# A mixture-of-experts FFN on one core: the hardware loops over experts and over weight tiles are written out

## The chip, the core and the metric

The kernel runs on one core of one Trainium2 chip. The metric is device time in microseconds of one execution; lower is better. A core has five engines that run their own instruction streams side by side and meet at semaphores: TensorE (PE, matrix multiplies), VectorE (DVE), ScalarE (ACT), GpSimd (POOL) and SyncE (SP, which here only issues transfers).

## What is computed

Each of 4096 tokens (512 wide) is rotated by a 4x4 quaternion product. A gate picks the best 2 of 8 experts, each expert takes at most 1024 tokens in order of arrival, and an expert is a two-layer FFN (512 to 2048 with relu, 2048 to 512). The weighted results are added to the input.

```python
xr = hamilton(q_left_n, hamilton(x_filtered, q_right_conj))      # spectral gate is a factor
scores = softmax(xr @ gate_w.T); topv, topi = top_k(scores, 2)
gates = topv / sum(topv)
loc = place of the token in its expert; valid = loc < cap         # cap = 1024
disp[topi * cap + loc] += xr * valid
h  = relu(einsum('ecd,ehd->ech', disp, fc1_w) + fc1_b)
eo = einsum('ech,ehd->ecd', h, fc2_w) + fc2_b
out = x + sum(eo[flat_idx] * gates * valid)
```

## The kernel before

**Two parts.** A straight part of about 105 us loads x, computes the gate, sorts tokens into the 8 x 1024 slots and prepares the first slab. Then comes the main part: 8 experts, in each 2 slabs of 512 slots (`half`), in each 16 steps (`hh`, one 128-row tile of the hidden layer). That is 256 steps in all, 32 to an expert.

**One step on PE.** Every product is done in three fp32r pieces (hi x hi, hi x lo, lo x hi). A step of PE is `fc1` for the step after it (12 matmuls into `hp`, lines 830 to 832) and then `fc2` for the step itself (12 matmuls into the accumulators `eo`, lines 842, 843 and 847). The very last step has only `fc2`. A matmul here is a weight load (PEld in the profile) and a multiply.

**The others in a step.** ACT turns `hp` into `h_hi` (line 448) and `h_full` (line 451), DVE makes `h_lo` of them (line 669). In 16 of the 32 steps of an expert ACT and DVE also prepare a weight tile two steps ahead: DVE turns it (`turn_tile`, line 656), ACT rounds it to `w1T_hi` and `w2_hi` (lines 438, 440), and DVE makes the remainders `w1T_lo` and `w2_lo` (lines 661, 664). After the last step of a slab DVE adds the four blocks of `eo` to `rows` (line 765), and POOL scatters them to `out` (line 385). POOL gathers the next slab's rows, ACT issues transfers that bring them through DRAM, and DVE rotates them.

**The loops.** PE, DVE, ACT and POOL each run the function `expert(e, last)` through the helper `experts` of lines 237 to 241: experts 0 to 6 in a hardware loop (`Fori`, a register counts `e`), and then expert 7 as straight code. So each of these four engines has six jumps back from the end of an expert to the start of the body, and one place, between experts 6 and 7, where it runs on into straight code. SP has a hardware loop of its own (line 278): the loads of weight tiles 2 to 127, two tiles to an iteration, each load waiting until its buffer is free (`w1_T`, `w2_ready`). Where a wait or an address depends on `e` or `m`, it is a register that an instruction (REGISTER_ALU) has computed; in straight code it is a constant.

**Order.** All orders are written out by hand and enforced by semaphores. Nothing in the kernel uses a scheduler.

Of the kernel before, what the change touches and what calls it, by code (L numbers as in the profile page):

```python
# [34 lines left out]
def program(nc, x, cond, q_right, spectral, gate_w, fc1_w, fc1_b, fc2_w, fc2_b, out):  # L35
    B, S, D = x.shape
    E, H, _ = fc1_w.shape
# [5 lines left out]
    HT = H // P  # L43
# [7 lines left out]
    RAW = 2  # L51
# [30 lines left out]
    with ctx:  # L82
# [153 lines left out]

        def experts(eng, body):

            with eng.Fori(0, E - 1) as e:
                body(e, False)  # L240
            body(E - 1, True)

        def load_cut(eng, to, rows_128, arrived, parts=range(P // BLK)):

            cut = rows_128.rearrange("(hq r) (k dq c) -> dq r k hq c", r=BLK, k=Q, c=BLK)
            for dq in parts:
                part = to[dq * BLK:(dq + 1) * BLK, :].rearrange("r (k hq c) -> r k hq c", k=Q, c=BLK)
                eng.dma_start(part, cut[dq]).then_inc(arrived, 16)  # L250
# [3 lines left out]
        @block.sync  # L254
        def _(sp):
            sp.dma_start(small[0:Q, :], cond).then_inc(small_in, 16)
            sp.dma_start(small[Q:2 * Q, :], q_right).then_inc(small_in, 16)
            sp.dma_start(small[2 * Q:2 * Q + 1, :], spectral.rearrange("a b c d -> (a b c) d")).then_inc(small_in, 16)
            sp.dma_start(gw_nat[:, :], gate_w).then_inc(gw_in, 16)
            for q in range(Q):  # L260
                sp.dma_start(x_all[:, 0:XC, q * P:(q + 1) * P], x_tiles[:, 0:XC, q * P:(q + 1) * P]).then_inc(x_in0[q], 16)
            sp.dma_start(b1_nat[:, :], fc1_b.rearrange("e a (t p) -> (e a t) p", p=P)).then_inc(b1_in, 16)
            for c in range(1, CHUNKS):
                tiles = slice(XC * c, XC * (c + 1))
                sp.dma_start(x_all[:, tiles, :], x_tiles[:, tiles, :]).then_inc(x_in[c][0], 16)
            def load_w1(row, c):

                load_cut(sp, w1_raw[:, c, :], w1_rows[ds(row, P), :], w1_in[c])

            for n in range(RAW):  # L270
                load_w1(n * P, n)
                sp.dma_start(w2_raw[:, n, :], w2_rows[n * P:(n + 1) * P, :]).then_inc(w2_in[n], 16)
            for c in range(CHUNKS):
                tiles = slice(XC * c, XC * (c + 1))
                for arrived in x_in[c]:
                    sp.wait_ge(arrived, 16)
                sp.dma_start(out_tiles[:, tiles, :], x_all[:, tiles, :]).then_inc(out_init, 16)
            with sp.Fori(1, E * HT // RAW) as m:
                for c in range(RAW):
                    sp.wait_ge(w1_T, RAW * m + (c - RAW + 1))  # L280
                    load_w1(m * (RAW * P) + c * P, c)
                    sp.wait_ge(w2_ready, RAW * m + (c - RAW + 1))
                    sp.dma_start(w2_raw[:, c, :], w2_rows[ds(m * (RAW * P) + c * P, P), :]).then_inc(w2_in[c], 16)

        @block.gpsimd
        def _(pool):
# [86 lines left out]
            def expert(e, last):  # L373
                for half in range(SLABS):
# [22 lines left out]
                    if not (last and half >= SLABS - 2):  # L397
                        gather_x(s + 2, half, 1)

            experts(pool, expert)  # L400

        @block.scalar
        def _(act):
# [68 lines left out]
            def expert(e, last):  # L472
                for half in range(SLABS):
                    for hh in range(HT):
# [15 lines left out]
                        if not end:  # L490
# [13 lines left out]
                            if hh in HI_AT:  # L504
                                split_y(s1, (half + 1) % 2, HI_AT.index(hh))

            experts(act, expert)

        @block.vector
        def _(dve):  # L510
# [218 lines left out]
            def expert(e, last):  # L729
                for half in range(SLABS):  # L730
                    s = e * SLABS + half
                    end = last and half == SLABS - 1
                    for hh in range(HT):
# [27 lines left out]
                        if hh == HT - 1:  # L761
                            for b in range(SB):
# [3 lines left out]
                                                         rows[:, b, :], ALU.mult, ALU.add).then_inc(sums_ready, 1)  # L766

            experts(dve, expert)

        @block.tensor  # L770
# [139 lines left out]
```

## Time and profile before

| | before |
|---|---|
| time, median of 3 runs | 1538.37 us (1534.41 to 1542.68) |
| span of the profiled execution | 1528.3 us |
| what lies around the span, median minus span | 10.1 us |
| PE busy | 1458.1 us, 95% of the span |
| DVE, ACT, POOL busy | 820.2, 537.3, 285.5 us (54%, 35%, 19%) |
| mean granted TensorE clock | 0.977 of full speed |
| instruction transfers | 69 packets on q8, 41 on q14 |

The profiled execution's own total time is not among the three; its span is from the first to the last instruction, and the median lies 10.1 us over it. The profile divides time by engine and by source line, and for each instruction it says how long its engine had sat idle before it and what ended that. "issue" there is time in which the engine waited for nothing that the profile shows. PE's records overlap, since matmuls are pipelined: one is 390 ns long, but one starts every 227 ns.

### The profile page before, as it was taken

What the parts mean: (1) busy time and instruction counts of PE and PEld (TensorE: products, weight loads), DVE (VectorE), ACT (ScalarE), POOL (GpSimd) and SP (SyncE); (2) the same over time, 40 slices, a digit from 0 to 9 for tenths busy, and PEclk for the clock granted to TensorE, in tenths of its full rate; (3) what the DMA queues carried; (4) which work ended last, traced back from release to release, by engine and by line L of the source; (5) the groups of instructions that cost most, each with busy time, mean ns of one, the idle gap of its engine ahead of it and who ended that gap; (6) DMA issues with size and microseconds to landing.
All of it is one profiled execution on the core that took longest, in us unless ns stands there. A gap on an engine that the chain in (4) does not pass through costs nothing.

```text
span 1528.3 us, 21024 instructions
## 1 busy us (share of the span) xinstructions
PE 1458.1 (95%) x6470; PEld 1196.0 (78%) x6470; DVE 820.2 (54%) x1484; ACT 537.3 (35%) x871; POOL 285.5 (19%) x342
## 2 busy tenths in 40 slices
PE   7569999999999999999999999999999999999996
PEld 5348888788887888788887888788887888888885
DVE  6756634575355824566345753568245662558311
ACT  4234422343233422344233432344223432344221
POOL 1040030301204031120303121130312103030301
PEclk9669999999999999999999999999999999999998
DMA  8456431774319732394318742296324943196100
GB/s 291 179 138 146 100 102 36 160 146 106 75 41 180 151 97 55 96 175 98 110 28 160 159 103 65 53 190 134 91 55 107 174 90 103 34 181 137 56 0 27
DMA packets 446304, 169.30 MB, mean 111 GB/s; under 512 B 405248, under 2 KB 407433, under 8 KB 444274
## 3 DMA queue, kind: packets, MB, share of 16 engines
q1 hardware_dynamic: 293218, 84.01, 25.7%
q0 software_dynamic: 18096, 52.35, 12.1%
q10 hardware_dynamic: 134880, 31.47, 10.1%
q8 instruction: 69, 1.13, 0.3%
q14 instruction: 41, 0.34, 0.1%
HBM read 127.00 MB, written 41.03 MB: 110 GB/s over the span
## 4 chain that ended last, share of the span: by engine, by line
PE 95%; DVE 2%; issue 1%; DMA 0%; POOL 0%; ACT 0%; SPq 0%; DVEq 0%; POOLq 0%
PE hp L831 15%; PE hp L830 15%; PE eo L843 15%; PE eo L842 15%; PE eo L847 15%; PE hp L832 15%; PE hp L855 1%; PE eo L805 1%; PE hp L787 1%; PE hp L788 1%; DVE y_half L713 0%; DVE x_turned L713 0%; DMA rows<-in_x,gather_row 0%; PE xp L794 0%; DVE yT_lo L698 0%
## 5 line engine op out<-in xcount | busy, mean ns | idle before, releaser
L669 DVE TENSOR_TENSOR h_lo<-h_full,h_hi 128x512 fp32r<-128x512 f32 x256 | 176.6, 690 | 537.7 <-ACT h_full L451 537.6
L831 PE MATMUL hp<-yT_lo,w1T_hi 128*128 128x512 f32 x1020 | 397.7, 390 | 16.3 <-issue 16.3
L830 PE MATMUL hp<-yT_hi,w1T_hi 128*128 128x512 f32 x1020 | 398.1, 390 | 0.4 <-issue 0.2
L842 PE MATMUL eo<-w_hi,h_hi 128*128 128x512 f32 x1024 | 398.3, 389 | 0.0
L843 PE MATMUL eo<-w_lo,h_hi 128*128 128x512 f32 x1024 | 398.3, 389 | 0.0
L832 PE MATMUL hp<-yT_hi,w1T_lo 128*128 128x512 f32 x1020 | 397.5, 390 | 0.0
L448 ACT ACTIVATE h_hi<-hp,b_now 128x512 fp32r<-128x512 f32 x256 | 176.1, 688 | 617.7 <-PE hp L832 613.0
L847 PE MATMUL eo<-w_hi,h_lo 128*128 128x512 f32 x1024 | 273.7, 389 | 0.0
L832 PEld LDWEIGHTS hp<-yT_hi,w1T_lo 128*128 128x128 f32 x1020 | 192.0, 188 | 57.3 <-issue 17.6
L830 PEld LDWEIGHTS hp<-yT_hi,w1T_hi 128*128 128x128 f32 x1020 | 191.8, 188 | 42.1 <-issue 2.4
L842 PEld LDWEIGHTS eo<-w_hi,h_hi 128*128 128x128 f32 x1024 | 192.3, 188 | 40.0
L847 PEld LDWEIGHTS eo<-w_hi,h_lo 128*128 128x128 f32 x1024 | 192.2, 188 | 39.9
L843 PEld LDWEIGHTS eo<-w_lo,h_hi 128*128 128x128 f32 x1024 | 192.2, 188 | 39.9
L831 PEld LDWEIGHTS hp<-yT_lo,w1T_hi 128*128 128x128 f32 x1020 | 191.9, 188 | 39.6
L438 ACT ACTIVATE w1T_hi<-w_turned 128x512 fp32r<-128x512 f32 x128 | 80.8, 631 | 273.3 <-DVE w_turned L656 258.3
L451 ACT ACTIVATE h_full<-hp,b_now 128x512 f32<-128x512 f32 x256 | 174.5, 682 | 0.0
L348 POOL DMA_INDIRECT x_blk<-in_x,gather_now x60 | 61.3, 1022 | 553.8 <-DVE x_turned L677 542.4
L385 POOL DMA_INDIRECT out<-rows,scatter_now x64 | 65.2, 1018 | 515.9 <-DVE rows L765 504.0
L692 DVE SCALAR_TENSOR_TENSOR y_half<-x_turned,rot,y_half 128x256 f32<-128x256 f32 x360 | 150.0, 478 | 0.0
L661 DVE TENSOR_TENSOR w1T_lo<-w_turned,w1T_hi 128x512 fp32r<-128x512 f32 x128 | 88.6, 693 | 92.4 <-ACT w1T_hi L438 92.4
L656 DVE STREAM_TRANSPOSE w_turned<-w_raw 128x512 f32<-128x512 f32 x126 | 88.7, 704 | 16.2 <-issue 9.5
L664 DVE TENSOR_TENSOR w_lo<-w_raw,w_hi 128x512 fp32r<-128x512 f32 x128 | 87.6, 684 | 10.2 <-ACT w_hi L440 10.1
(146 smaller groups left out, 717.0 us busy)
## 6 DMA issues: line engine op xcount, KB each, us to landing
w_raw<-in_L_ffn_fc_w SPq DMA_DIRECT2D x512, 64.0 KB
w_raw<-in_L_ffn_fc_w SPq DMA_DIRECT2D x128, 256.0 KB, 3.1
slots_dram<-x_blk ACTq DMA_DIRECT2D x30, 512.0 KB, 3.6
x_blk<-slots_dram ACTq DMA_DIRECT2D x240, 64.0 KB
out<-x_all SPq DMA_DIRECT2D x8, 1024.0 KB, 12.3
x_all<-in_x SPq DMA_DIRECT2D x7, 1024.0 KB, 13.9
b_bc<-in_L_ffn_fc_b POOLq DMA_DIRECT2D x8, 256.0 KB
x_all<-in_x SPq DMA_DIRECT2D x4, 256.0 KB, 4.1
```

Of the source, the lines that this page charges most:

```text
L448: act.activation(h_hi[:, c, :], hp[:, c, :], ACT.Relu, bias=b1_now[:, hh:hh + 1]).then_inc(h_hi_ready, 1)
L451: act.activation(h_full[:, :], hp[:, c, :], ACT.Relu, bias=b1_now[:, hh:hh + 1]).then_inc(h_full_ready, 1)
L656: dve.transpose(w1_turned[:, c, :, :].rearrange("p q n -> p (q n)"), w1_raw[:, c, :]).then_inc(w1_T, 1)
L661: dve.tensor_tensor(w1T_lo[:, hh, :, :], w1_turned[:, c, :, :], w1T_hi[:, hh, :, :].bitcast(F32), ALU.subtract).then_inc(w1_ready, 1)
L669: dve.tensor_tensor(h_lo[:, c, :], h_full[:, :], h_hi[:, c, :].bitcast(F32), ALU.subtract).then_inc(h_ready, 1)
L692: ins = dve.scalar_tensor_tensor(y, x_turned[:, :, j, :], rot[:, i, j:j + 1], y, ALU.mult, ALU.add)
L830: pe.matmul(bank, w1T_hi[:, hh, q, :], yT_hi[:, par, q, :], start=(q == 0), stop=False)
L831: pe.matmul(bank, w1T_hi[:, hh, q, :], yT_lo[:, par, q, :], start=False, stop=False)
L832: ins = pe.matmul(bank, w1T_lo[:, hh, q, :], yT_hi[:, par, q, :], start=False, stop=(q == Q - 1))
L842: pe.matmul(eo[:, b, :], h_hi[:, c, blk], w2_hi[:, hh, :], start=(hh == 0), stop=False)
L843: pe.matmul(eo[:, b, :], h_hi[:, c, blk], w2_lo[:, hh, :], start=False, stop=False)
L847: pe.matmul(eo[:, b, :], h_lo[:, c, blk], w2_hi[:, hh, :], start=False, stop=(hh == HT - 1)).then_inc(fc2_done, 1)
```

## The change

The two `Fori` loops become Python loops, so that the program holds the body of every expert on every one of the four engines, and the 63 iterations of SP's loads. Order, buffers and waits are the same; wait values and addresses that were registers are constants. Straight code has no branch in the main part.

```diff
         def experts(eng, body):
 
-            with eng.Fori(0, E - 1) as e:
+            for e in range(E - 1):
                 body(e, False)
             body(E - 1, True)
...
-            with sp.Fori(1, E * HT // RAW) as m:
+            for m in range(1, E * HT // RAW):
                 for c in range(RAW):
                     sp.wait_ge(w1_T, RAW * m + (c - RAW + 1))
                     load_w1(m * (RAW * P) + c * P, c)
```

On PE, where an expert's body ends and the next begins, before (the two L239 rows are the loop counter and the jump; the rows behind them are the straight code of expert 7, and the jump's target starts with the same matmuls):

```order
L844 REGISTER_ALU
L847 MATMUL eo<-w2_hi,h_lo 128x512 x4
L239 REGISTER_ALU
L239 COMPARE_AND_BRANCH
L830 MATMUL hp<-yT_hi,w1T_hi 128x512
L831 MATMUL hp<-yT_lo,w1T_hi 128x512
```

and the same place now, as it stands at every expert:

```order
L842 MATMUL eo<-w2_hi,h_hi 128x512
L843 MATMUL eo<-w2_lo,h_hi 128x512
L847 MATMUL eo<-w2_hi,h_lo 128x512 x4
L830 MATMUL hp<-yT_hi,w1T_hi 128x512
L831 MATMUL hp<-yT_lo,w1T_hi 128x512
```

No matmul moved; the jump and the register instructions are gone. On DVE, at the same place of the program, before:

```order
L763 REGISTER_ALU
L764 REGISTER_ALU
L765 SCALAR_TENSOR_TENSOR rows<-eo,gate_now,rows 128x512
L239 REGISTER_ALU
L239 COMPARE_AND_BRANCH
L656 STREAM_TRANSPOSE w1_turned<-w1_raw 128x512
L661 TENSOR_TENSOR w1T_lo<-w1_turned,w1T_hi 128x512
```

and now:

```order
L669 TENSOR_TENSOR h_lo<-h_full,h_hi 128x512
L765 SCALAR_TENSOR_TENSOR rows<-eo,gate_now,rows 128x512 x4
L656 STREAM_TRANSPOSE w1_turned<-w1_raw 128x512
L661 TENSOR_TENSOR w1T_lo<-w1_turned,w1T_hi 128x512
```

The four sums of a slab and the turn of the next expert's third weight tile now follow each other without a jump. The program's PE code grows from 1,860 to 6,468 matmuls, DVE's, ACT's and POOL's code by a factor of about 2.5, and SP's from 44 to 664 transfers.

## Rows read from the trace of the kernel before

**Rows 1.** The page, part 1: busy time, share and instructions of each engine

```profile
PE 1458.1 (95%) x6470; PEld 1196.0 (78%) x6470; DVE 820.2 (54%) x1484; ACT 537.3 (35%) x871; POOL 285.5 (19%) x342
```

**Rows 2.** The page, part 4: the chain that ended last, by engine

```profile
PE 95%; DVE 2%; issue 1%; DMA 0%; POOL 0%; ACT 0%; SPq 0%; DVEq 0%; POOLq 0%
```

**Rows 3.** Waits: engine and line, releaser, us in total, times, longest

```profile
ACT h_hi L448 <- PE hp L832: 613.0, 224, 4.2
...
PE hp L831 <- issue: 16.3, 6, 2.9
...
DVE w_turned L656 <- issue: 9.5, 6, 1.8
...
DVE w_turned L656 <- DMA w_raw<-in_L_ffn_fc_w: 6.7, 6, 2.2
```

**Rows 4.** Timeline of PE, first jump back (start, us, what, idle before)

```profile
278.07 1.07 PE L847 MATMUL eo<-w_hi,h_lo 128*128 128x512 f32 x4
...
280.02 0.40 PE L830 MATMUL hp<-yT_hi,w1T_hi 128*128 128x512 f32 x1
282.82 0.59 PE L831 MATMUL hp<-yT_lo,w1T_hi 128*128 128x512 f32 x1 [2.40 <-issue]
283.20 0.63 PE L832 MATMUL hp<-yT_hi,w1T_lo 128*128 128x512 f32 x1
...
288.01 1.07 PE L847 MATMUL eo<-w_hi,h_lo 128*128 128x512 f32 x4
```

**Rows 5.** Timeline of PE, second jump back

```profile
456.65 1.07 PE L847 MATMUL eo<-w_hi,h_lo 128*128 128x512 f32 x4
457.87 0.49 PE L830 MATMUL hp<-yT_hi,w1T_hi 128*128 128x512 f32 x1
...
461.95 0.39 PE L831 MATMUL hp<-yT_lo,w1T_hi 128*128 128x512 f32 x1 [2.89 <-issue]
...
465.59 0.62 PE L847 MATMUL eo<-w_hi,h_lo 128*128 128x512 f32 x2
```

**Rows 6.** Timeline of PE: step 0, and experts 6 to 7, run on without a jump

```profile
109.43 1.07 PE L847 MATMUL eo<-w_hi,h_lo 128*128 128x512 f32 x4
...
1343.10 1.07 PE L847 MATMUL eo<-w_hi,h_lo 128*128 128x512 f32 x4
1344.01 0.39 PE L830 MATMUL hp<-yT_hi,w1T_hi 128*128 128x512 f32 x1
...
1349.44 0.39 PE L830 MATMUL hp<-yT_hi,w1T_hi 128*128 128x512 f32 x1
...
1514.46 1.07 PE L847 MATMUL eo<-w_hi,h_lo 128*128 128x512 f32 x4
```

**Rows 7.** Stretches: us, busy of PE, PEld, DVE, ACT, POOL, granted clock, DMA share, GB/s

```profile
278.00:292.00 14.00, 11.51 (x44) 8.87 (x43) 7.89 (x12) 3.65 (x7) 6.13 (x8) 0.88 0.70 195
292.00:1515.00 1223.00, 1208.71 (x5327) 999.00 (x5326) 645.75 (x1149) 432.03 (x698) 230.65 (x255) 1.00 0.48 104
```

**Rows 8.** DMA queues, stretch 459.3 to 461 us: packets, MB, share of 16 engines

```profile
q8 instruction: 1, 0.02, 4.3%
```

**Rows 9.** DMA queues, stretch 1343 to 1515 us, expert 7

```profile
q8 instruction: 6, 0.10, 0.2%
q14 instruction: 3, 0.02, 0.1%
```

**Rows 10.** Timeline of DVE, second jump back

```profile
457.18 2.73 DVE L765 SCALAR_TENSOR_TENSOR rows<-eo,gate_now,rows 128x512 f32<-128x512 f32 x4
461.51 0.71 DVE L656 STREAM_TRANSPOSE w_turned<-w_raw 128x512 f32<-128x512 f32 x1 [1.61 <-issue]
```

**Rows 11.** Timeline of DVE, experts 6 to 7, run on without a jump

```profile
1343.62 2.73 DVE L765 SCALAR_TENSOR_TENSOR rows<-eo,gate_now,rows 128x512 f32<-128x512 f32 x4
1346.27 0.70 DVE L656 STREAM_TRANSPOSE w_turned<-w_raw 128x512 f32<-128x512 f32 x1
1347.67 0.69 DVE L661 TENSOR_TENSOR w1T_lo<-w_turned,w1T_hi 128x512 fp32r<-128x512 f32 x1 [0.70 <-ACT w1T_hi L438]
```

**Rows 12.** Timeline of SP's queue and of DVE, one load and what frees its buffer

```profile
446.15 0.70 DVE L656 STREAM_TRANSPOSE w_turned<-w_raw 128x512 f32<-128x512 f32 x1
...
447.04 2.89 SPq L250 DMA_DIRECT2D w_raw<-in_L_ffn_fc_w  x4
```

## The prediction

> **What bounds the kernel now.** I read the busy times first, then the chain that ended last, then PE's waits, and then PE's timeline around the places where the loop jumps back. PE is busy 1458.1 us of a span of 1528.3 [rows 1], and the chain is PE for 95% [rows 2]. So the only time to be had without removing matmuls is time in which PE stands. In the main part PE has exactly one kind of wait: before line 831, "issue", 6 times, 16.3 us together, 2.9 at the longest [rows 3]. Six is the number of jumps back. All six stand at the same place: four matmuls into the first step of the next expert, and not at a semaphore, since line 831 is the second piece of an `fc1` that is already under way. ACT, by contrast, waits for PE's `hp` in 224 of 256 steps, 613.0 us together [rows 3]: it has spare time nearly everywhere, and so has DVE.
>
> **What the jumps cost, from PE's step.** "Idle" understates it, so I count by the period of a step. The L847 groups of step 0 and step 31 start at 109.43 and 278.07 [rows 4, 6]: 168.64 us for 31 steps, 5.440 us each. Expert 7, which is straight code already, shows the same: from the L847 of step 223 (1343.10) to that of step 255 (1514.46) there are 171.36 us [rows 6], which is 32 x 5.440 less the 2.72 of the `fc1` that the last step lacks, to the hundredth. In between, from step 31 (278.07) to step 223 (1343.10), there are 192 steps: 192 x 5.440 = 1044.5, but they take 1065.0. The surplus is **20.5 us**, over the six jumps, 3.4 each. It has three parts.
> - The idle time itself, 16.3.
> - At the first jump the granted clock is 0.88 on average over 14 us [rows 7], and the matmuls right after the pause are 0.63 us long instead of 0.39 [rows 4]. This step pair takes 288.01 - 278.07 = 9.94, that is 4.50 over 5.44, of which 2.40 is idle. Most of the other 2.1 is the slow clock. In the 1223 us after that, with five more jumps, the clock is 1.00 [rows 7].
> - At the other jumps a few tenths around the pause: the second takes 465.59 - 456.65 = 8.94, that is 3.50 over a step, of which 2.89 is idle; the first matmul behind the jump starts 1.22 after the L847 group instead of 0.91 [rows 5, 6]. I take 2.1 for all five, what is left of the 20.5.
>
> **What the pause is.** In the stretch of 1.7 us that lies within the second pause one packet of 16 KB (0.02 MB) moves on an instruction queue, q8 [rows 8]. I read this as PE's next piece of code: the jump goes to code that is no longer, or only in part, on hand; the first eight instructions (four loads and four multiplies) are there, the next piece is asked for only when it is needed, and PE stands meanwhile. In expert 7 the same queue brings 6 packets in 172 us, one each 28.7, and PE does not pause once [rows 6, 9]. Straight code is evidently fetched ahead.
>
> [...]
>
> **The change, part by part.**
> - *PE's jumps go.* Gain 20.5 us, all of it on the path, if each expert's start now looks like that of expert 7: L847 at 1343.10, `fc1` at 1344.01, 0.91 later, as in any step [rows 6].
> - *PE's register instructions go.* They lie under matmuls; steps are 5.440 us long in the loop and in straight code alike. Gain 0.
> - *PE's code gets longer.* Six more copies of the body, each 32 x 5.440 = 174 us long, are 1044 us of it; at a packet each 172 / 6 = 28.7 us that is some 36 packets. The loop already took such packets while it ran (q8 is used in all experts), and PE's only pauses were the six at the jumps. Cost 0 as in expert 7; the bound above is that of rival D.
> - *DVE's, ACT's and POOL's jumps go.* DVE stands 6 times for 9.5 us together at its jump [rows 3], for instance 1.61 at 461.51 [rows 10]. These lie beside PE's pause and bring nothing by themselves. They matter for what follows: once PE no longer pauses, what these engines do at an expert's start must be in time by itself.
> - *What is late next.* The tightest place is the third weight tile of an expert. DVE may turn it only behind the four sums of the slab. Between experts 6 and 7, where nobody jumps, the sums run from 1343.62 to 1346.35, the turn starts at 1346.27, and `w1T_lo` is done at 1347.67 + 0.69 = 1348.36 [rows 11]. The `fc1` that reads it starts at 1349.44 [rows 6]. The margin is 1.08 us, and PE did not wait. The six other boundaries get this same margin. I cost this at 0; the cover is those 1.08 us, and if it is gone (a weight load that comes late: DVE waited for one 6 times, 2.2 us at most [rows 3]) it costs the excess, up to 1.1 us a time. Expert 7 has less to do than others, but the boundary's own work (sums, tile, `h_hi`, stores) is the same.
> - *SP's loop goes.* The first load of an iteration is issued at 447.04, when DVE's turn that frees its buffer ended at 446.85 [rows 12]; the jump of SP lies within waiting time. Gain 0. No load starts earlier in the step than now, since each still waits for DVE's turn, so no new collisions of transfers.
> - *Head and tail.* The straight part of 105 us and the last 14 us after PE's last step have no loop and stay.
>
> Sum: 0 + 20.5 off the span, 1528.3 - 20.5 = 1507.8. The median stands 10.1 over the span, which nothing here touches: **1517.9 us**, 1.3% faster. The pauses differ between jumps (the shortest and longest of the rows shown are 2.40 and 2.89), and the slow clock behind the first one need not be there in every run: from 16.3 + 2.1 without it to some 24 with a second such case, 1514 to 1520. The three runs spread over 8.3 us, half a per cent, so 1514 to 1522 is the forecast's own range.
>
> **Rivals.**
> - *B, the margin at the boundary does not hold.* For it: 1.08 us is little, and DVE waited up to 2.2 for a weight load. Against it: the one straight boundary showed no wait, and those 6 waits for loads never reached PE. Price up to 2.2 - 1.08 = 1.1 at six boundaries, 6.7 together: 1518 to 1524.6.
> - *C, the pause is not the jump's.* Something at an expert's boundary other than the jump holds PE, or straight code brings its own pause at the same place. Then nothing changes: 1538. Against it: the boundary at 1343.10 has the same work and no pause. [...]
> - *D, slower.* PE's code does not arrive ahead of need once all of it is straight. The place is the end of each piece of 28.7 us; the price at most that of a jump's pause, 2.7 (16.3 / 6), for 36 new pieces: 97 us, and 1615 in the worst case. It outweighs the gain from 20.5 / 36 = 0.57 us a piece. For it: nothing in the rows but that transfers of code share the 16 DMA engines with data, and those are 48% busy in the main part [rows 7]. Against it: six pieces in expert 7 without a pause.
>
> **How the numbers follow.** Forecast (all 20.5, within its spread) 0.78; B 0.12; C 0.05, with the branch-price reading another 0.02; D 0.03. What this kernel's measurement can tell from no change is about 0.5%, 7.7 us: forecast and B lie beyond it (0.90 faster), C within it (0.07), D slower (0.03). The time is the forecast's, 1517.9. The range takes the forecast's spread and B: 1513 to 1525; C and D, 0.10 together, stay out.
>
> **What would show it.** Right: PE's wait "issue" before line 831 gone from the waits; a distance of 1384.5 us between the first and the last L847 group (255 x 5.440 less 2.72; now 1405.0); a span near 1508; a granted clock of 1.00 from 105 us to the end of PE's work; fewer packets on q8 than now, about 1390 / 28.7 = 48 for the main part. B shows as waits of PE for DVE's `w1T_lo` at line 830 at the experts' starts. C shows as the same six pauses; D as short "issue" waits each 28.7 us, or long steps at that distance. The forecast is wrong if PE's step leaves 5.44 us, or if a slower start eats the gain: the first L847 group should still start near 109.4.

## The result and the profile after

| | before | after |
|---|---|---|
| time, median | 1536.39 us (1531.74 to 1542.68, 4 runs) | 1510.70 us (1508.79 to 1511.23, 4 runs) |
| ratio after to before, 95% interval | | 0.9834 [0.9801, 0.9868] |
| span of the profiled execution | 1528.3 us | 1509.3 us |
| mean granted TensorE clock | 0.977 | 0.977 |
| instruction packets on q8, on q14 | 69, 41 | 52, 35 |
| idle time of PE at the starts of experts | 16.3 us, six times | none |

The change makes the kernel 1.7% faster. The sign and the mechanism of the forecast hold. The time does not: 1517.9 was forecast, the range began at 1513, and 1510.7 was measured. The spread is new as well: before ran over some 11 us, after over 2.4.

The page of the kernel after, its part 1 and two lines of its part 3, answering to [rows 1] and [rows 9]:

```profile
PE 1455.4 (96%) x6470; PEld 1196.7 (79%) x6470; DVE 819.8 (54%) x1484; ACT 537.2 (36%) x871; POOL 283.5 (19%) x342
...
q8 instruction: 52, 0.85, 0.2%
q14 instruction: 35, 0.29, 0.1%
```

PE's timeline (start, us, what, idle before): the first and the last L847 group, answering to [rows 6], and the matmuls at the first expert boundary, answering to [rows 4].

```profile
111.00 1.07 PE L847 MATMUL eo<-w_hi,h_lo 128*128 128x512 f32 x4
...
285.08 1.07 PE L847 MATMUL eo<-w_hi,h_lo 128*128 128x512 f32 x4
285.99 0.39 PE L830 MATMUL hp<-yT_hi,w1T_hi 128*128 128x512 f32 x1
...
1495.48 1.07 PE L847 MATMUL eo<-w_hi,h_lo 128*128 128x512 f32 x4
```

From the first group to the last there are 1384.48 us; the prediction had 1384.5 for 255 steps without a pause. No step of the main part is longer than 5.44 us. The stretches (us, busy of PE, PEld, DVE, ACT, POOL, granted clock, DMA share, GB/s) say the same, answering to [rows 7]:

```profile
278.00:292.00 14.00, 14.00 (x63) 11.59 (x63) 9.25 (x14) 6.44 (x11) 5.03 (x6) 1.00 0.77 198
...
105.00:1495.00 1390.00, 1390.00 (x6127) 1151.16 (x6127) 746.44 (x1328) 499.89 (x808) 255.71 (x287) 1.00 0.48 105
```

PE is busy in all 1390 us of the main part. The boundary work on DVE, answering to [rows 11], here for experts 0 to 1:

```profile
280.07 2.73 DVE L765 SCALAR_TENSOR_TENSOR rows<-eo,gate_now,rows 128x512 f32<-128x512 f32 x4
282.71 0.70 DVE L656 STREAM_TRANSPOSE w_turned<-w_raw 128x512 f32<-128x512 f32 x1
284.11 0.69 DVE L661 TENSOR_TENSOR w1T_lo<-w_turned,w1T_hi 128x512 fp32r<-128x512 f32 x1 [0.70 <-ACT w1T_hi L438]
```

`w1T_lo` is done at 284.80 and PE reads it from 285.99 on: a margin of 1.19 us. It is 1.18 or 1.19 at all seven boundaries, so rival B did not happen.

The span fell by 19.0 us, not by the 20.5 that went from the steps, because the main part began 1.57 us later (first group at 111.00 instead of 109.43). The straight part differed: the second half of its first `fc1` began 0.35 us later (102.16 for 101.81), and the clock rose later. Before, a matmul of the first full `fc1` took 0.39 us from 105.33 on (first line); after, matmuls were still 0.63 us long at 107.45 (the others):

```profile
105.33 0.39 PE L832 MATMUL hp<-yT_hi,w1T_lo 128*128 128x512 f32 x1
...
106.17 0.63 PE L830 MATMUL hp<-yT_hi,w1T_hi 128*128 128x512 f32 x1
107.45 0.63 PE L830 MATMUL hp<-yT_hi,w1T_hi 128*128 128x512 f32 x1
108.46 0.40 PE L830 MATMUL hp<-yT_hi,w1T_hi 128*128 128x512 f32 x1
```

This start belongs to the execution, not to the change: in a second profile of the changed kernel (`after_again`) the first L847 group starts at 109.19, and the distance to the last is 1384.47 again.

### The profile page after: what moved, and what is told of

It is laid out like the page before. It is cut to its first block, busy times and chain, and to the rows that moved or that the text cites. A ratio compares the mean times of both kernels' runs of the same rounds, so it can differ in the third digit from the quotient of the medians.

```text
span 1509.3 us, 17949 instructions
## 1 busy us (share of the span) xinstructions
PE 1455.4 (96%) x6470; PEld 1196.7 (79%) x6470; DVE 819.8 (54%) x1484; ACT 537.2 (36%) x871; POOL 283.5 (19%) x342
## 4 chain that ended last, share of the span: by engine, by line
PE 96%; DVE 2%; DMA 1%; POOL 0%; ACT 0%; issue 0%; SPq 0%; DVEq 0%; POOLq 0%
PE eo L842 15%; PE eo L843 15%; PE eo L847 15%; PE hp L830 15%; PE hp L831 15%; PE hp L832 15%; PE hp L855 1%; PE eo L805 1%; PE hp L787 1%; PE hp L788 1%; DMA rows<-in_x,gather_row 0%; DVE x_turned L713 0%; POOL rows L321 0%; POOL out L385 0%; PE xp L794 0%
## 5 line engine op out<-in xcount | busy, mean ns | idle before, releaser
L847 PE MATMUL eo<-w_hi,h_lo 128*128 128x512 f32 x1024 | 273.7, 389 | 0.0
L847 PEld LDWEIGHTS eo<-w_hi,h_lo 128*128 128x128 f32 x1024 | 192.3, 188 | 39.7
L385 POOL DMA_INDIRECT out<-rows,scatter_now x64 | 69.0, 1079 | 517.0 <-DVE rows L765 505.2
## 6 DMA issues: line engine op xcount, KB each, us to landing
out<-x_all SPq DMA_DIRECT2D x8, 1024.0 KB, 11.6
```

The source lines that it names most:

```text
L847: pe.matmul(eo[:, b, :], h_lo[:, c, blk], w2_hi[:, hh, :], start=False, stop=(hh == HT - 1)).then_inc(fc2_done, 1)
```

## Experiments

Theory at the start: the whole gain is PE's six pauses for code and the slow clock behind them. The rival: what was missed lies with the other engines' loops, or outside the span. Three sets of four kernels follow; those of a set ran on one chip beside the kernel of before, whose medians there were 1534.89 (23 runs), 1531.75 (7) and 1532.31 us (7). Every kernel without pauses of 2 us repeats within 5 us, so I compare these by their times. The changed kernel ran beside the first set alone, and the start of the main part moves by up to 2.3 us between executions (first L847 group at 108.74 to 111.00), so a difference of 1 or 2 us between sets means little by itself.

A measure without this is the *surplus*: by how much the distance from the first to the last L847 group, in the profiled execution, is over the 1384.5 us of 255 even steps. It is 20.5 and 22.4 us in the two profiles of before, 21.6 in `others_only`, 9.5 in `head232`, 9.0 in `pair`, 6.3 in `head208`, 4.6 in `pe_only`, 2.7 in `hint`, 2.3 in `head0`, 2.2 in `dve_loop`, and 0.0 in the two profiles of after, in `rest_loop` and in `head0_dve`.

### Before, again: where its spread comes from

The kernel is unchanged.

> The kernel of before, unchanged, for the time and clock of each of its executions. The forecast missed by 5 us on the side of the gain although the span of the profiled execution fell by 19.0, near the 20.5 that was summed. Theory T (clock after a pause): executions of before differ because each of the six pauses may or may not be followed by a few us at the half clock; then span and mean granted clock move together: spans from about 1528 (clock 0.977, one slow stretch behind a pause) up to about 1541 (clock near 0.970, five or six slow stretches of 3.4 us, some 2 us each), and time minus span is the same 1.9 us as in the executions of after. Theory S (outside the span): spans are all near 1528 with clock 0.977, and time minus span varies from 3 to 14 us.

Measured: 1533.93 us (1531.85 to 1542.28, 12 runs), ratio 1.0001 [0.9980, 1.0021]. Theory S is refuted: in all 35 executions of before on that chip, and in every other execution whose span is on record (101 in all), time minus span is 1.6 to 2.1 us. The spans themselves range from 1527.3 to 1540.3. So the profiled execution of the prediction, with a span of 1528.3, took about 1530.2 us, an estimate from its span, since its time isn't on record: it was one of the fastest of this kernel. The "10.1 us around the span" set it against three other executions.

Theory T holds in part. The two executions at clock 0.971 took 1540.6 and 1542.3 us, the three at 0.977 took 1529.2, 1531.6 and 1533.4. In this kernel's profile two of the six pauses are followed by a slow stretch, in the earlier one it was one: a granted clock of 0.50 for 3.4 us, there from 282.8 to 286.1 us, here in 814.2 to 817.5 and 995.1 to 998.4 (windows; columns as above):

```profile
812.00:826.00 14.00, 11.32 (x45) 9.20 (x44) 6.91 (x11) 4.84 (x8) 7.75 (x10) 0.88 0.73 197
990.00:1004.00 14.00, 10.78 (x42) 8.60 (x41) 6.16 (x10) 4.44 (x8) 6.88 (x10) 0.88 0.68 203
```

But executions at clock 0.975 run from 1529.2 to 1540.2, so something besides the clock varies. The same profile shows one such thing, a few steps behind the fifth pause: SP's and ACT's transfers stand for some microseconds, ACT stands 6.4 us before an `h_hi`, and PE, which is hardly ever caught up with, waits for it. One step then takes 5.96 us (1016.06 - 1010.10) instead of 5.44, and the `fc1` behind it waits for its weight tile.

```profile
1010.10 1.07 PE L847 MATMUL eo<-w_hi,h_lo 128*128 128x512 f32 x4
1014.16 0.47 PE L842 MATMUL eo<-w_hi,h_hi 128*128 128x512 f32 x1 [0.27 <-ACT h_hi L448]
...
1016.06 1.07 PE L847 MATMUL eo<-w_hi,h_lo 128*128 128x512 f32 x4
1017.38 0.50 PE L830 MATMUL hp<-yT_hi,w1T_hi 128*128 128x512 f32 x1 [0.26 <-DVE w1T_lo L661]
```

The two steps add 1.1 of the 22.4 us of surplus. How often this happens I can't say from single profiles.

### After, again

The kernel is the changed one.

> The changed kernel once more, beside the others on the same chip. Both theories: median 1508 to 1512 us, ratio to before 0.980 to 0.987. Theory T: no pause, so no slow stretch in the main part, clock 0.977 in every execution and a spread of 3 us at most. Theory S would let it spread as before does, by 8 us or so, since what lies outside the span is the same in both kernels.

Measured: 1510.31 us (1509.41 to 1510.47, 6 runs), ratio 0.9833 [0.9807, 0.9858], clock 0.977 to 0.978. As T expected: without pauses there is neither a slow stretch nor a spread.

### PE alone, and all but PE

```diff
-            with eng.Fori(0, E - 1) as e:
-                body(e, False)
+            if eng.engine == mybir.EngineType.PE:
+                for e in range(E - 1):
+                    body(e, False)
+            else:
+                with eng.Fori(0, E - 1) as e:
+                    body(e, False)
             body(E - 1, True)
```

The second kernel has `!=` in place of `==`, and SP's loop over weight tiles is written out in it.

> Only PE's loop over experts is written out; DVE, ACT, POOL and SP keep their hardware loops. Theory P (the gain is PE's own pauses): the whole gain, 1509 to 1516 us, ratio 0.980 to 0.988; at experts' starts DVE still stands 1.5 to 1.8 us, which eats the 1.08 to 1.19 us of margin of the third weight tile, so PE should wait 0.3 to 0.7 us for w1T_lo at line 830 at each of six boundaries, 2 to 4 us together: 1512 to 1515. Theory Q (the pauses come from all engines jumping at once or from shared queues): at most half the gain, 1523 or more.

Measured: 1514.39 us (1512.67 to 1516.88, 4 runs), ratio 0.9862 [0.9827, 0.9896]. As theory P says, but the 4.1 us to the changed kernel are a cost of the others' loops, which the prediction had at 0. By the surplus it is 4.63 us: 2.17 at the third tile behind the six jumps, and 2.46 at later steps of three experts (more on them at `rest_loop`). DVE's timeline at the first boundary (lines are 4 higher in this kernel):

```profile
278.71 2.73 DVE L769 SCALAR_TENSOR_TENSOR rows<-eo,gate_now,rows 128x512 f32<-128x512 f32 x4
282.52 0.71 DVE L660 STREAM_TRANSPOSE w_turned<-w_raw 128x512 f32<-128x512 f32 x1 [1.09 <-issue]
283.94 0.69 DVE L665 TENSOR_TENSOR w1T_lo<-w_turned,w1T_hi 128x512 fp32r<-128x512 f32 x1 [0.70 <-ACT w1T_hi L442]
```

`w1T_lo` is done at 284.63, and PE's `fc1` starts 0.05 us behind it, 1.05 instead of 0.91 after its L847 group at 283.63:

```profile
283.63 1.07 PE L851 MATMUL eo<-w_hi,h_lo 128*128 128x512 f32 x4
284.68 0.50 PE L834 MATMUL hp<-yT_hi,w1T_hi 128*128 128x512 f32 x1
```

The margin is gone: PE starts 0.05 or 0.06 us behind the tile at all six jumps. At each of DVE's jumps here three packets of code (8 KB each) arrive on q14. The stretch 278 to 284 us of `rest_loop`, where ACT and POOL jump and DVE's code is straight, has none. This is the same stretch of `dve_loop`, where DVE alone jumps:

```profile
q14 instruction: 3, 0.02, 1.3%
```

So DVE's stand at its jump looks like a fetch of code too. No run moved the head of DVE's loop to test it.

> DVE, ACT, POOL and SP are written out, PE keeps its hardware loop. Theory P: no gain, 1531 to 1541 us, ratio 0.995 to 1.003, six pauses of 2.3 to 3.0 us in the first fc1 of each expert as before. Theory Q: the pauses shrink or vanish, and half of the gain or more appears, 1525 or less.

Measured: 1530.43 us (1527.39 to 1531.73, 10 runs), ratio 0.9966 [0.9948, 0.9984]. PE's jumps keep nearly everything, as P says, but there is a small gain beyond P's range, 4.5 us against the 1534.89 of before. PE's pauses are still six, and shorter: 11.6 us together instead of 16.3. But four of them, not one or two, are followed by 3.4 us at the half clock, and the surplus of this profile is 21.6 us, no less than before. It is the slowest of the ten executions, so the profile doesn't show where the gain of the median lies.

```profile
PE hp L835 <- issue: 11.6, 6, 2.1
```

The two halves add up. PE's loop costs 1530.43 - 1510.31 = 20.1 us, the others' loops 1514.39 - 1510.31 = 4.1, together 24.2, and before minus after is 1534.89 - 1510.31 = 24.6. The 95% interval on each of these differences is 3 to 5 us wide either way, so the sum fits, and proves no more than that. Once PE does not pause, the others' loops cost through a late weight tile. While it pauses, they may cost through the length of its pause; that is not shown in time, as the profile above says. I see no reason why both should come to 4 us.

### The same loop on PE, at another place in the code

```diff
-            with eng.Fori(0, E - 1) as e:
+            PE = mybir.EngineType.PE
+            if eng.engine == PE:
+                with nc.Fori(0, E - 1, engines=bass.OrderedEngineSet([PE]), head_slot={PE: 0}) as e:
+                    body(e, False)
+            else:
+                with eng.Fori(0, E - 1) as e:
```

The others keep their loops. A piece of code is here what one packet of q8 brings: all 52 packets of after are of 16,384 bytes, and between its 4th (131.2 us) and its 52nd (1469.1) the trace has 12,296 PE instructions, 256.2 a packet. `head_slot` asks for the loop's first instruction at a given one of these 256 slots. That it lands there shows in `head232` below: PE comes to stand behind the loop's first 24 instructions (11 weight loads, 11 matmuls and two of registers), and 232 + 24 = 256. In before there are 11 of them (five loads, four matmuls, two of registers), so its head is near slot 245.

> The kernel of before, with PE's hardware loop only moved: its first instruction is loaded at the first slot of a 16 KB piece of code (256 slots) instead of some eight slots before a piece's end. Jumps, waits and work stay. Theory F (two fetches in a row: the jump asks for the piece with the loop's head, which PE's queue of waiting matmuls nearly covers; eight instructions later the next piece is asked for, and this one is bare): the pause of 2.3 to 3.0 us in the first fc1 goes, at most 0.6 us remains at each jump, time 1515 to 1520. Theory J (a jump costs its pause wherever it lands): as before, 1533 to 1538.

The trace of before fits F's two fetches in a row. PE's branch back (COMPARE_BRANCH, L239) lasts 3.75 us in the median of its seven records, 4.07 at the longest. At the first jump it starts at 275.02 and lasts 3.95, with one packet on q8 in 275 to 279.1 us. It lies under matmuls that stand ahead of it in the program: 17 of them start after it does, 0.227 us apart, the last at 278.75. The first one behind the jump starts at 279.23, 1.16 after the L847 group instead of 0.91. Then comes the pause, with a second packet in 279.2 to 282.9.

Measured: 1512.13 us (1511.66 to 1512.59, 4 runs), ratio 0.9869 [0.9850, 0.9887]. Theory J falls: the same six jumps, and no pause (PE's timeline at the first, lines 5 higher here):

```profile
278.23 1.07 PE L852 MATMUL eo<-w_hi,h_lo 128*128 128x512 f32 x4
279.13 0.39 PE L835 MATMUL hp<-yT_hi,w1T_hi 128*128 128x512 f32 x1
...
279.81 0.39 PE L835 MATMUL hp<-yT_hi,w1T_hi 128*128 128x512 f32 x1
280.04 0.39 PE L836 MATMUL hp<-yT_lo,w1T_hi 128*128 128x512 f32 x1
```

It is even better than F expected. PE's branch back now lasts 0.21 us in the median of the jumps, and q8 shows why:

```profile
q8 instruction: 15, 0.25, 0.1%
```

15 packets in the whole run. The trace of after holds 13,470 PE instructions (matmuls, weight loads and 530 others) in 52 packets: about 259 a packet. The trace of before holds 13,898, of which 1,661 make one pass of the loop. Without the six further passes 3,932 are left, which makes 15.2 packets. So each piece was fetched once, and six further passes through the loop ran from what PE held. The original fetched the loop again on each pass: 54 of its 69 packets fall between 240 and 1320 us, the time of the six jumps, nine to a pass.

```profile
q8 instruction: 54, 0.88, 0.4%
```

In `head0` one falls in this time. What is left over the changed kernel, 2.3 us of surplus and 1.8 us by the medians, is DVE's jump: the steps at the third tile last 5.70 to 5.90 us instead of 5.44.

> As head0, but the loop's first instruction stands at slot 232: 24 slots, some 12 matmuls and 2.7 us of PE's work, before the end of the piece. Theory F: the pause moves to behind the 11th or 12th matmul and shrinks by the 1.8 us of work that now lie ahead of it, to 0.5 to 1.2 us, six times: 1518 to 1526. Theory J: as before, 1533 to 1538.

Measured: 1519.01 us (1518.70 to 1519.89, 4 runs), ratio 0.9916 [0.9897, 0.9934], 70 packets. The pause has moved to behind the 11th matmul and shrunk, in total to 5.4 us in six (waits, then the first one in PE's timeline; lines are 5 higher here). The six steps with it have 9.1 us of surplus.

```profile
PE hp L837 <- issue: 5.4, 6, 1.3
...
282.67 0.51 PE L837 MATMUL hp<-yT_hi,w1T_lo 128*128 128x512 f32 x1 [1.03 <-issue]
```

None of these six is followed by a slow clock. As F expected, in place and size: PE runs to the piece's end, 24 instructions behind slot 232, and stands there 0.7 to 1.3 us.

```diff
-            with eng.Fori(0, E - 1) as e:
+                with nc.Fori(0, E - 1, engines=bass.OrderedEngineSet([PE]), hint_back_edge=True) as e:
```

PE's loop, its head not moved by `head_slot`, gets one more instruction at its start, in the trace a BRANCH_PREFETCH_HINT of 31 ns (median of 7, one a pass).

> [...] Theory J: as before, 1533 to 1538.

Measured: 1511.76 us (1511.20 to 1512.63, 4 runs), ratio 0.9868 [0.9849, 0.9887], 15 packets. Theory J falls here too: no fetch was needed at the jumps, and PE's branch back lasts 0.22 us in the median, not 3.75. I think that with this instruction in the loop the piece behind the loop's end is not fetched and so pushes nothing out. The packets of q8 fit that: `hint` has none between 240 and 1320 us, where `head0` has one and before 54. No run tests this apart, and whether the loop's head stayed where it was in before is not shown either.

> Before, with PE's loop head at slot 208 of a piece, 48 slots (24 matmuls, 5.4 us of work) before its end. The runs so far: with the head at slot 0 PE's code was brought in 15 packets in all (before 69) and no pause was left; at slot 232 in 70 packets, with pauses of about 0.9 us. The body of some 1,590 instructions touches 7 pieces from slot 0 and 8 from slot 208 or 232. Theory H (PE holds 8 pieces and always brings the next one too: 7 + 1 fit, 8 + 1 push out the head's piece, and then each piece in turn): some 69 packets again, but the second fetch is now asked for 5.4 us of work ahead, so no pause: 1512 to 1514. Theory K (code is held whatever its place, and the head's slot only sets the pause): about 15 packets, 1512 to 1514. Theory L (each refetched piece costs, so the packets are the price): 69 packets and 1518 or more.

Measured: 1516.20 us (1515.53 to 1516.97, 4 runs), ratio 0.9891 [0.9863, 0.9920], 70 packets. The packets are as H says and K is refuted; the time is 2 us above H and 2 below L. PE's code pause is gone (0.3 us in all), and what it waits for now is DVE's tile:

```profile
PE hp L835 <- DVE w1T_lo L666: 2.4, 6, 1.0
PE hp L835 <- issue: 0.3, 2, 0.2
```

Five of the six waits, 1.5 us, are for the third tile, behind DVE's own jump. The sixth is the longest, 0.96 us, and has another cause: the seventh tile of an expert, whose load DVE itself had awaited for 3.19 us.

```profile
656.75 0.71 DVE L661 STREAM_TRANSPOSE w_turned<-w_raw 128x512 f32<-128x512 f32 x1 [3.19 <-DMA w_raw<-in_L_ffn_fc_w]
658.91 0.50 PE L835 MATMUL hp<-yT_hi,w1T_hi 128*128 128x512 f32 x1 [0.96 <-DVE w1T_lo L666]
```

The 6.3 us of surplus are about 1.6 in the six first steps (5.54 to 5.92 us), 3.5 in the steps of the third tile and 1.3 in that one late load. The third tile is later here than with the head at slot 0 because DVE stands longer at its jump: 1.34 to 1.95 us, 1.6 on average, against 1.06 to 1.25, 1.2 on average. The same split runs through all kernels that keep DVE's jump. Where PE fetches its loop again, DVE stands 1.5 to 1.8 us on average (both profiles of before, `head232`, `head208`, `pair`); where PE does not, 1.1 or 1.2 (`pe_only`, `head0`, `hint`, `dve_loop`). That the two fetches hinder each other fits this; no run tests it.

### Fewer jumps, and the others one by one

```diff
-            with eng.Fori(0, E - 1) as e:
+            with eng.Fori(0, E - 2, 2) as e:
                 body(e, False)
-            body(E - 1, True)
+                body(e + 1, False)
+            body(E - 2, False)
+            body(E - 1, True)
```

> Two experts to an iteration of each engine's loop over experts (0 to 5 in three iterations, 6 and 7 straight), SP's loop as before: two jumps instead of six, heads where they were. If the gain of the change is a price per jump, a third of it stays: 1510.3 + 24.6 / 3 = 1518.5, within 1516 to 1521, with two pauses of 2.3 to 3.0 us. If it is the register instructions, the number of iterations of SP's loop or anything that lies in the steps, the time stays above 1525.

Measured: 1519.36 us (1518.23 to 1520.11, 4 runs), ratio 0.9911 [0.9881, 0.9940]. A third of the jumps keeps about a third of the loss, with two pauses:

```profile
PE hp L833 <- issue: 4.9, 2, 2.5
PE hp L832 <- DVE w1T_lo L663: 1.5, 1, 1.5
```

Of the 9.0 us of surplus 7.1 are in the two steps with the pauses, 3.6 each as in before. The other 1.8 are that one wait for `w1T_lo`, in the middle of an expert, behind a load that DVE had awaited for 4.82 us, and no part of a jump's own price.

> All written out except DVE's loop over experts. The forecast had costed the loops of the others at 0; together they measured 4.1 us (1514.39 with them, 1510.31 without). Theory D (DVE's own jump, 1.5 to 1.8 us behind the four sums, makes the third weight tile late): nearly all of that, 1512.5 to 1515, with PE waiting for w1T_lo at the third tile of each expert. Theory O (the loads that SP, ACT and POOL issue late are what counts): 1510 to 1511.5.

Only DVE's loop is kept. Measured: 1512.10 us (1511.16 to 1512.47, 4 runs), ratio 0.9867 [0.9848, 0.9886]. 1.8 us over the changed kernel, a little under D's range. The third tile of each expert is ready 0.06 us before PE starts on it at all six jumps, instead of 1.19. So PE starts as soon as it is there, and the steps last 5.65 to 5.86 us.

> PE and DVE written out; ACT, POOL and SP keep their loops. Theory D (of the others only DVE's jump costs, by the third weight tile): as the changed kernel, 1509.5 to 1511.5, no wait of PE for w1T_lo. Theory O (loads and activations late after the jumps of SP, ACT and POOL): up to 2.3 us more, that is what lies between dve_loop (1512.10) and pe_only (1514.39): 1512 to 1513.

Only PE and DVE are written out. Measured: 1509.78 us (1509.36 to 1510.12, 4 runs), ratio 0.9849 [0.9821, 0.9878]. The loops of ACT, POOL and SP by themselves cost nothing, and no step of PE is over 5.44 us. Together with DVE's they cost 2.3 us more than DVE's alone where PE's code is straight (1514.39 against 1512.10), and nothing more where PE's head is at slot 0 (1512.13). The surplus puts the difference at 2.46 us (4.63 and 2.17). It lies in three experts of `pe_only`: in two PE waited for the seventh weight tile (steps of 6.00 and 5.88 us), in the third it stood inside an `fc1` at 652 us with no releaser shown (a step of 6.50). Late steps of this kind, away from the jumps, stand in `before_again`, `dve_loop`, `hint`, `pair`, `head208` and `head232` too, but not in `head0` and in none of the four profiles where neither PE pauses nor DVE jumps. Whether the others' jumps bring them about is not settled.

> PE keeps its hardware loop with the head at slot 0, DVE is written out, ACT, POOL and SP keep their loops. If the whole gain of the change is two things, PE's fetch pauses and DVE's jump ahead of the third weight tile, this kernel with one sixth of the added PE code reaches the changed kernel: 1509.5 to 1511.5. If straight code on PE brings anything else (registers, waits), it stays 1 us or more above.

PE loops with its head at slot 0, DVE is written out, the rest loops. Measured: 1510.16 us (1508.81 to 1510.61, 4 runs), ratio 0.9851 [0.9822, 0.9880], no step over 5.44 us. That is the changed kernel's time with PE's code as small as before. No version beats it: PE has no idle time left in the main part, so both stand at its floor.

## Why the prediction was right, and where it was wrong

**Right.**
- The bound and the place: PE, and in PE the six pauses in the first `fc1` of an expert.
- "Straight code is evidently fetched ahead": no pause in 52 packets; D is refuted.
- The surplus in the steps of the profiled execution, 20.5 us: the distance of the L847 groups came out at 1384.48 for 1384.5.
- The cause, a fetch of code: shown by moving the loop's head. With the head at slot 0 the jumps stay and the pauses go; at slot 232 they move to the 11th matmul. C is refuted.
- That a jump need not cost a pause: `head0` keeps all of PE's jumps and shows no idle time at them. The forecast also gave 0.02 to a reading that takes the branch's own price as all that a jump costs. No run shows the price that it used; what the runs show in its place is 0.21 to 0.24 us for each of the six branches back in `head0`, under matmuls, and a result of 1510.7 us where this reading ended at no change. The 2.7 us of a pause are the fetch.
- B: the margin of the third tile is real, and it held. Its mechanism appeared in the kernels that leave DVE's loop in place.

**Wrong: the step from the span to the time.** "The median stands 10.1 over the span, which nothing here touches." Only 1.9 us lie around a span, in all executions. The other 8.2 were the difference between the profiled execution and the median of three others, whose spans are not on record. Their times, 1534.41 to 1542.68, lie where those of the 35 do (1529.16 to 1542.28). With 1.9 the same sum gives 1507.8 + 1.9 = 1509.7, within 1.0 of the 1510.7 measured. The spread of before, which I took for measurement noise on both sides, was a property of the kernel that the change removes.

**Wrong in size: what the loops cost in a typical execution.** The term was 20.5 us. It measures 24.6 (1534.89 to 1510.31). The profiled execution was a lucky one, with a slow clock behind one pause of six. (The interval on 24.6, from the ratio, is 21.8 to 29.6. Before's medians on the two other chips are about 3 us lower.) The mean clock of the 35 executions is 0.9744 where that one had 0.977. One slow stretch of about 3.4 us takes 0.0011 off the mean (3.4 / 1530 / 2). The difference of 0.0022 (unrounded, 0.97666 less 0.97443) is therefore two more stretches. A jump's step with one takes 7.5 us without its idle time, a step without one 5.8 (means of the 18 steps in the profiles of before, `before_again` and `others_only`): 1.7 us each, 3.3 of the 4.1. This is an estimate from means. The rest may be of the late-transfer kind seen in `before_again`, and is not measured apart.

**Wrong: "DVE's, ACT's and POOL's jumps go ... bring nothing by themselves", and SP's "Gain 0".** By themselves they bring 4.1 us (`pe_only` to after) or 4.5 (before to `others_only`), one sixth of the gain. The prediction had both facts, DVE standing 1.61 us at its jump and a margin of 1.08 for the tile that follows, and costed the pair at 0 because PE's own pause covered it. Once the pause is gone, the 1.03 to 1.27 us for which DVE stands in `pe_only` and `head0` use up the margin, and the steps at the third tile grow by 2.2 or 2.3 us together. It did not ask either what the others' jumps do to the length of that pause: 16.3 us in six with them, 11.6 without. SP's, ACT's and POOL's part alone is 0, as forecast.

**A reading that was too narrow.** "The jump goes to code that is no longer, or only in part, on hand" is true of this binary, not of this loop: with the head at slot 0 the body stayed in PE's store (one packet on q8 between 240 and 1320 us). What the count of packets fits is a store of eight pieces that always takes in the next one as well: 7 + 1 fit, 8 + 1 push out the piece that is needed next. The 1,661 instructions of a pass touch seven pieces of 256 from slot 0 and eight from slot 208, 232 or about 245 (before, by the 11 instructions ahead of its pause). (The some 1,590 that were expected give the same seven and eight.) The 15, 70 and 70 packets at slots 0, 208 and 232 are measured, and so are the nine a pass in before; the eight is my reading of them. By nine a pass the head's own piece was fetched again too, so the prediction's "the first eight instructions are there" holds only in that PE did not stand for them.

## What to carry to other kernels

When an engine with a long loop body idles a few us near each loop start with no releaser, count its instruction packets against the size of its code: if they exceed it, first try another place for the loop's head or the instruction of `hint`, since either did for PE here what writing its loop out does (1512.1 and 1511.8 us with the others' loops kept, against 1514.4). Cost the jumps of the engines that are not the bound together with the margin of what they produce next. And take the time of the profiled execution itself, not the distance of its span from a median: a kernel that pauses has a spread of its own, and a single profile may be its best case.

## What the runs showed of the hardware that I had not expected

- PE can run a body of 1,661 instructions seven times from its own store (15 packets in all); the same body with its head at slot 208 or 232 of a piece is fetched on every pass (70 packets).
- The price of a missing piece is about 2.7 us of idle time when eight instructions of work lie ahead of it, 0.9 when 11 matmuls do, and next to none with 24 matmuls. In the length of the step it is 3.4, 1.5 and 0.3 us on average.
- A pause of PE of 1.8 to 3.2 us is sometimes followed by 3.4 us at the half clock (granted 0.50): 1 and 2 of 6 in the two profiles of before, 4 of 6 in `others_only`, 1 of 2 in `pair`, none of 6 with pauses of 0.9 us. Which pauses it follows is open.
- With the other engines' jumps at the same moment PE's pause is 2.7 us on average, without them 1.9 (one profile). DVE's stand at its own jump is 1.5 to 1.8 us on average where PE fetches its loop again, and 1.1 or 1.2 where it does not.
